# A four-layer transformer kernel: projections split on two engines, fewer query transfers, and turnings in another order

## The reference

```python
# layers 0, 1 and 3 (norms and gates differ a little)
x = x + gate1 * proj(self_attention(ln(x)))
x = x + proj(cross_attention(q=x_or_ln(x), kv=context))
x = x + gate2 * mlp(ln(x))
# layer 2, a router over three experts
nx = ln(x); q = nx @ Wq; k = context @ Wk; v = context @ Wv
weights = softmax(q @ k.T * 128 ** -0.5)
evidence = weights @ v
combined = concat(nx, evidence, cond)
x = x + sigmoid(gate(combined)) * out(sum_e prob_e * expert_e(combined))
```

## Time and profile before

| | us |
|---|---|
| median of 3 runs | 6248.7 (6243.0 to 6251.5) |
| the profiled execution | 6255.5 |
| its span, first to last instruction | 6253.2 |
| mean granted TensorE clock | 0.881 |

### The profile page before, as it was taken

How to read it: one execution, slowest core, us unless ns; L and a number is a source line. 1 busy time by engine, 2 the same in 40 slices (tenths; PEclk the granted TensorE clock), 3 DMA queues, 4 the chain that set the end, 5 groups by cost and what they waited for, 6 DMA issues and landing times. The chain is left out here.

```text
span 6253.2 us, 151177 instructions
## 1 busy us (share of the span) xinstructions
PE 5213.4 (83%) x64126; PEld 3352.7 (54%) x64126; DVE 3844.1 (61%) x7732; ACT 3016.4 (48%) x4479; POOL 1458.3 (23%) x758
## 2 busy tenths in 40 slices
PE   4838999999985849999999877779675799999998
PEld 3614555555653615666666545555353466666664
DVE  4537888888744527777777623334353577777773
ACT  2324666666652315666666532212322366666665
POOL 2024444444302022333222000000201223332220
PEclk7667999999996669999999977779766799999999
DMA  3325545555403345555555211110141555555540
GB/s 76 63 64 156 158 157 164 164 164 158 147 17 65 64 110 162 165 164 165 164 167 164 73 33 48 48 38 1 44 77 28 171 165 165 165 164 164 164 152 15
DMA packets 544827, 717.59 MB, mean 115 GB/s; under 512 B 183450, under 2 KB 457402, under 8 KB 531770
## 3 DMA queue, kind: packets, MB, share of 16 engines
q1 hardware_dynamic: 535322, 696.87, 38.4%
q10 hardware_dynamic: 8832, 11.07, 0.8%
HBM read 441.82 MB, written 264.09 MB: 113 GB/s over the span
## 5 line engine op out<-in xcount | busy, mean ns | idle before, releaser
L1247 DVE TENSOR_REDUCE maxima<-ps 100x1 f32<-100x482 f32 (+1 forms) x4608 | 2720.2, 650 | 896.3 <-PE ps L1092 886.6
L1202 ACT ACTIVATE probs<-ps 128x800 f32<-128x800 f32 (+1 forms) x2304 | 1800.5, 835 | 655.6 <-PE ps L1113 653.9
L1092 PE MATMUL ps<-kst,qst 48*100 48x482 bf16 (+1 forms) x4608 | 1117.7, 411 | 107.1 <-DMA qst<-cross_q_parts 51.3
L1299 POOL TENSOR_TENSOR kparts<-kf,zero 128x1444 bf16<-128x1444 f32 x192 | 498.3, 2595 | 2280.3 <-ACT kf L1174 2250.9
L1130 PE MATMUL ps<-probs,vals 128*9 128x100 f32 x36864 | 1012.4, 250 | 7.9 <-ACT probs L1202 0.8
L1113 PE MATMUL ps<-qst,kst 128*128 128x200 bf16 (+1 forms) x9216 | 999.6, 250 | 11.7 <-DMA qst<-nparts 5.5
L1113 PEld LDWEIGHTS ps<-qst,kst 128*128 128x128 bf16 (+1 forms) x9216 | 759.0, 98 | 251.2 <-issue 124.7
L1130 PEld LDWEIGHTS ps<-probs,vals 128*9 128x9 f32 x36864 | 734.3, 90 | 259.6 <-issue 219.2
L1092 PEld LDWEIGHTS ps<-kst,qst 48*100 48x100 bf16 x4608 | 341.7, 119 | 630.2 <-DVE maxima L1247 329.9
L1180 ACT ACTIVATE vals<-ps 128x512 f32<-128x512 f32 (+1 forms) x288 | 161.9, 562 | 467.1 <-PE ps L1075 467.1
L1064 PE MATMUL ps<-ident,ctok 128*128 128x128 f32 (+1 forms) x1152 | 195.6, 292 | 210.2 <-DMA ctok<-in_ctx_dram 108.7
(11 more groups left out here) (256 smaller groups left out, 4951.3 us busy)
## 6 DMA issues: line engine op xcount, KB each, us to landing
kst<-ctx_k_stack SPq DMA_DIRECT2D x96, 2888.0 KB
ctx_k_stack<-kparts SPq DMA_DIRECT2D x192, 541.5 KB
ctx_k_stack<-kparts SPq DMA_DIRECT2D x192, 361.0 KB
ctok<-in_ctx_dram SPq DMA_DIRECT2D x96, 704.0 KB
ctx_k_stack<-kparts SPq DMA_DIRECT2D x192, 180.5 KB
c<-in_ctx_dram SPq DMA_DIRECT2D x32, 704.0 KB
o_sums<-osb SPq DMA_DIRECT2D x96, 200.0 KB
qst<-cross_q_parts SPq DMA_DIRECT2D x1152, 12.5 KB
```

The costliest lines, as they stand in the source:

```text
L1092: nc.tensor.matmul(ps[0:N, at:at + w], g.qst[s][row0:row0 + CROWS, j, N * e:N * e + N], g.kst[s][row0:row0 + CROWS, j, a:a + w], start=Tru ...
L1202: nc.scalar.activation(probs[kt % 2][hf][0:kts[kt], :].rearrange("p (k n) -> p k n", k=2), src, ACT.Exp).then_inc(exp_done, 1)
L1247: nc.vector.reduce_max(maxima[:, col:col + 1], ps[0:N, at:at + widths[c]], AX.X).then_inc(m_read, 1)
L1299: return nc.gpsimd.tensor_tensor(out, src, g.zero[0:src.shape[0], 0:1].to_broadcast(list(src.shape)), ALU.add)
```

## The change

It has three parts.

1. The splitting. A class `Split` says which chunks are "banked". Banked chunks are scaled in place in their PSUM bank and subtracted there by VectorE (rest to the bank, low to `parts[:, 2]`); the others go through `sq` and GpSimd as before. In a stage with two projections the first has no banked chunk and the second has all eight; in a stage with one projection the even chunks are banked. VectorE and ScalarE interleave the steps by chunk: VectorE scaling of c, rest of c - 1, low of c - 2; ScalarE high of c, middle of c - 1. GpSimd does the rest of a chunk and then the low part of the one before. The second projection no longer waits for the low parts of the first.
2. The query transfers. `cross_q_parts` gets the shape (8 chunks, 2, 3, 64, 400), and SyncE stores two transfers per chunk, 16 in a stage. The loads of cross attention read each batch's 100 columns out of rows of 400.
3. The router attention. The turning of context and weights is taken out of `pe_scores` and `pe_evidence`. TensorE's order per batch becomes: weights groups 0 and 1 of b, context groups 0 and 1 of b + 2, weights group 2, context group 2, evidence of b, scores of b + 2. The order on the other engines stays.

```diff
+class Split:
+    def __init__(self, sem, i, banked, parts, f):
+        self.banked, self.parts, self.f = banked, parts, f
+        self.f_ready, self.high, self.middle = sem(f"proj_read{i}"), sem(f"high{i}"), sem(f"middle{i}")
...
+    def value(self, g, c):
+        return bank(g, c) if c in self.banked else tok(self.f, c)
...
+def dve_split(g, dve, s, full, bias, scale):
+    for c in range(NCH + 2):
+        if c < NCH:
+            dve.wait_ge(full, c + 1)
+            g.nc.vector.tensor_scalar(s.value(g, c), bank(g, c), bias, scale, ALU.add, ALU.mult).then_inc(s.f_ready, 1)
+        if 0 <= c - 1 < NCH and c - 1 in s.banked:
+            dve.wait_ge(s.high, c)
+            g.nc.vector.tensor_tensor(bank(g, c - 1), bank(g, c - 1), s.part(0, c - 1), ALU.subtract).then_inc(s.dve_rest, 1)
+        if 0 <= c - 2 < NCH and c - 2 in s.banked:
+            dve.wait_ge(s.middle, c - 1)
+            g.nc.vector.tensor_tensor(s.part(2, c - 2), bank(g, c - 2), s.part(1, c - 2), ALU.subtract).then_inc(s.dve_low, 1)
+
+
+def act_split(g, act, s):
+    for c in range(NCH + 1):
+        if c < NCH:
+            act.wait_ge(s.f_ready, c + 1)
+            g.nc.scalar.activation(s.part(0, c), s.value(g, c), ACT.Copy).then_inc(s.high, 1)
+        if c:
+            act.wait_ge(s.rest(c - 1), s.nth(c - 1))
+            g.nc.scalar.activation(s.part(1, c - 1), s.value(g, c - 1), ACT.Copy).then_inc(s.middle, 1)
+
+
+def pool_split(g, pool, s):
+    copied = [c for c in range(NCH) if c not in s.banked]
+    for c, before in zip(copied + [None], [None] + copied):
+        if c is not None:
+            pool.wait_ge(s.high, c + 1)
+            g.nc.gpsimd.tensor_tensor(tok(s.f, c), tok(s.f, c), s.part(0, c), ALU.subtract).then_inc(s.pool_rest, 1)
+        if before is not None:
+            pool.wait_ge(s.middle, before + 1)
+            g.nc.gpsimd.tensor_tensor(s.part(2, before), tok(s.f, before), s.part(1, before), ALU.subtract).then_inc(s.pool_low, 1)
...
-    per = CH // N
     for c in range(NCH):
-        sp.wait_ge(low, c + 1)
+        sp.wait_ge(split.low(c), split.nth(c))
         for e in range(2):
-            for j in range(per):
-                b = c * per + j
-                sp.dma_start(g.qx[b, e].rearrange("t r n -> r t n"),
-                             parts[HALF * e:HALF * e + HALF, :, N * b:N * b + N]).then_inc(stored, 16)
-    sp.wait_ge(stored, 16 * 2 * B)
+            sp.dma_start(g.qx[c, e].rearrange("t r n -> r t n"),
+                         parts[HALF * e:HALF * e + HALF, :, CH * c:CH * c + CH]).then_inc(stored, 16)
+    sp.wait_ge(stored, 16 * 2 * NCH)
...
+        banked = [(), tuple(range(NCH))] if npart == 2 else [tuple(range(0, NCH, 2))]
+        splits = [Split(sem, i, banked[i], parts[i], sq) for i in range(npart)]
...
+            per = CH // N
             for e in range(2):
                 for part, (first, copies) in enumerate(Q_SLOTS):
+                    src = g.qx[b // per, e, part].rearrange("(d j) n -> d j n", j=PAIRS)[:, :, N * (b % per):N * (b % per) + N]
                     for slot in range(first, first + copies):
                         at = QHALF * e + HD * slot
-                        sp.dma_start(g.qst[s][at:at + HD, :, N * e:N * e + N],
-                                     g.qx[bass.ds(b, 1), e, part].rearrange("a (d j) n -> (a d) j n", j=PAIRS)).then_inc(qst_loaded[s], 16)
+                        sp.dma_start(g.qst[s][at:at + HD, :, N * e:N * e + N], src).then_inc(qst_loaded[s], 16)
...
+                for b in range(B):
+                    k, k2 = known(b), known(b + 2) if b + 2 < B else None
+                    for t in range(2):
+                        pe_turn_weights(pe, k, t)
+                    if k2 is not None:
+                        for t in range(2):
+                            pe_turn_context(pe, k2, t)
+                    pe_turn_weights(pe, k, 2)
+                    if k2 is not None:
+                        pe_turn_context(pe, k2, 2)
+                    pe_evidence(pe, k)
+                    if k2 is not None:
+                        pe_scores(pe, k2)
```

More of the change, by code:

```diff
@@ L163, in act_shift @@
         g.nc.scalar.activation(tok(xn, b, N), tok(xn, b, N), ACT.Identity, bias=add[:, bass.ds(b, 1)]).then_inc(modulated, 1)
-def act_split(g, act, f, parts, f_ready, high, rest, middle):
-    for c in chunks(act):
-        act.wait_ge(f_ready, c + 1)
-        g.nc.scalar.activation(parts[:, 0, bass.ds(c * CH, CH)], tok(f, c), ACT.Copy).then_inc(high, 1)
-    for c in chunks(act):
-        act.wait_ge(rest, c + 1)
-        g.nc.scalar.activation(parts[:, 1, bass.ds(c * CH, CH)], tok(f, c), ACT.Copy).then_inc(middle, 1)
@@ L176, in pool_split @@
-def pool_split(g, pool, f, parts, high, rest, middle, low):
-    for c in chunks(pool):
-        pool.wait_ge(high, c + 1)
-        g.nc.gpsimd.tensor_tensor(tok(f, c), tok(f, c), parts[:, 0, bass.ds(c * CH, CH)],
-                                  ALU.subtract).then_inc(rest, 1)
-    for c in chunks(pool):
-        pool.wait_ge(middle, c + 1)
-        g.nc.gpsimd.tensor_tensor(parts[:, 2, bass.ds(c * CH, CH)], tok(f, c),
-                                  parts[:, 1, bass.ds(c * CH, CH)], ALU.subtract).then_inc(low, 1)
@@ L188, in sp_parts_out, with part, nth, rest @@
-def sp_parts_out(g, sp, parts, dram, low, stored):
+class Split:
+    def __init__(self, sem, i, banked, parts, f):
+        self.banked, self.parts, self.f = banked, parts, f
+        self.f_ready, self.high, self.middle = sem(f"proj_read{i}"), sem(f"high{i}"), sem(f"middle{i}")
+        self.dve_rest, self.pool_rest = sem(f"dve_rest{i}"), sem(f"pool_rest{i}")
+        self.dve_low, self.pool_low = sem(f"dve_low{i}"), sem(f"pool_low{i}")
+    def part(self, k, c):
+        return self.parts[:, k, CH * c:CH * c + CH]
+    def value(self, g, c):
+        return bank(g, c) if c in self.banked else tok(self.f, c)
+    def nth(self, c):
+        return len([x for x in range(c + 1) if (x in self.banked) == (c in self.banked)])
+    def rest(self, c):
+        return self.dve_rest if c in self.banked else self.pool_rest
+    def low(self, c):
+        return self.dve_low if c in self.banked else self.pool_low
@@ L395, in project_phase @@
         full = [sem(f"proj_full{i}") for i in range(npart)]
-        f_ready = [sem(f"proj_read{i}") for i in range(npart)]
-        high = [sem(f"high{i}") for i in range(npart)]
-        rest = [sem(f"rest{i}") for i in range(npart)]
-        middle = [sem(f"middle{i}") for i in range(npart)]
-        low = [sem(f"low{i}") for i in range(npart)]
+        banked = [(), tuple(range(NCH))] if npart == 2 else [tuple(range(0, NCH, 2))]
+        splits = [Split(sem, i, banked[i], parts[i], sq) for i in range(npart)]
         stored = [sem(f"stored{i}") for i in range(npart)]
@@ L421, in _ @@
                     pe_linear(g, pe, [w], [lambda c: tok(xin, c)], xin_ready, xin_per, free, full[i])
-                    free = f_ready[i]
+                    free = splits[i].f_ready
             @block.vector
@@ L435, in _ @@
                 for i, (w, bias, dram, scale) in enumerate(projections):
-                    for c in chunks(dve):
-                        dve.wait_ge(full[i], c + 1)
-                        if i:
-                            dve.wait_ge(low[i - 1], c + 1)
-                        nc.vector.tensor_scalar(tok(sq, c), bank(g, c), bias, scale, ALU.add,
-                                                ALU.mult).then_inc(f_ready[i], 1)
+                    dve_split(g, dve, splits[i], full[i], bias, scale)
             @block.scalar
@@ L453, in _ @@
                 for i in range(npart):
-                    act_split(g, act, sq, parts[i], f_ready[i], high[i], rest[i], middle[i])
+                    act_split(g, act, splits[i])
             @block.gpsimd
@@ L458, in _ @@
                 for i in range(npart):
-                    pool_split(g, pool, sq, parts[i], high[i], rest[i], middle[i], low[i])
+                    pool_split(g, pool, splits[i])
             @block.sync
@@ L464, in _ @@
                     if dram is g.qx:
-                        sp_queries_out(g, sp, parts[i], low[i], stored[i])
+                        sp_queries_out(g, sp, parts[i], splits[i], stored[i])
                     else:
-                        sp_parts_out(g, sp, parts[i], dram, low[i], stored[i])
+                        sp_parts_out(g, sp, parts[i], dram, splits[i], stored[i])
 class attention_close_sems:
```

59 lines of the change are left out of this document (28 added, 31 removed).

## The result

The changed kernel takes 6003.2 us (median of 4 runs, 5998.3 to 6009.0) against 6249.8 for the kernel before in the same session: ratio 0.9608, 95% interval 0.9591 to 0.9624. That is 247 us less, where 221 was forecast. The profiled executions took 6255.5 and 6009.0 us, spans 6253.2 and 6007.2, so 246.0 us are to be found in the traces.

| stretch | before | after | gained | forecast |
|---|---|---|---|---|
| three query stages | 164.1 | 56.3 | 107.9 | 110 |
| three self projection stages | 105.7 | 92.3 | 13.4 | 6 |
| router attention, first query copy to the next block's first product | 502.5 | 378.4 | 124.1 | 105 |
| everything else | | | 0.6 | 0 |

The account below looks back on a forecast made before the run. Bounds named: SyncE's issuing queue in query stages, GpSimd in self stages, a chain through TensorE in the router. Gains of 110 + 6 + 105 = 221 us from 6248.7 gave 6028 us, range 5985 to 6105.

Parts of the forecast that it names:

- Part 1: Query stages: 16 transfers and the new split take three stages from 164.1 to 54.3 us, gain 110 (99 to 119).
- at 1.0 to 1.3 us a chunk the queue keeps up: Query stages: SyncE's issues, 0.51 to 0.65 us each, keep pace with the split, which is late next.
- 4.14: Query stages: us from the last transfer's start to the stage's end, taken from the self stage.
- Part 2: Self projection stages: VectorE alone splits the second projection; gain 2.2 us each, 6 in all (bounds -6 and 12).
- Part 3: Router attention: slot 10.5 us at full clock, 11.7 with the clock's cost; gain 105 us (46 to 144).
- clock surcharge: Router attention: the mean slot's 3.20 us above full clock falls to 1.2, bounds 0 to 3.20.
- The load that the move exposes: Router attention: TensorE waits some 0.8 us for the context's load, hidden at full clock behind the stall for VectorE's copy.
- Part 4: Cross attention's query loads: strided reads issue in the same 0.646 us; no change, bounds -0.1 and +0.1 us an issue.
- (a): Router attention: the order helps but the clock costs the same; slot 13.7, gain 46, total 6087 us; chance 0.17.
- (b): Router attention: the clock falls in every slot; slot 16.1, 24 us lost, total 6157 us; chance 0.11.
- (c): Cross attention: SyncE issues strided query loads more slowly; at 1.6 us an issue, total 6527 us; chance 0.03.
- (d): Splits: part 2 gains nothing, part 1 its lower bound; 17 us less, total 6045; chance 0.67 together with the forecast.

Follow-up runs that it names:

- The run with eight transfers: The changed kernel with both self projections split by alternate chunks between VectorE and GpSimd, and one query transfer per chunk: 5978.3 us, ratio 0.9560 to before.
- copies first: The kernel before, with VectorE copying a batch's turned weights ahead of the maximum over the next batch's scores: 6114.2 us, ratio 0.9776.
- gap filled: The kernel before with two needless products per router slot in TensorE's 1.75 us wait: 6153.4 us; with ten needless turnings instead: 6172.1 us.
- a fourth buffer: The changed kernel with a fourth context buffer in the router attention, so contexts load a slot earlier: 6036.5 us, ratio 0.9647 to before.
- a third less of it: The changed kernel with a fourth context buffer and one needless product per slot behind the context's second group: 6038.0 us, ratio 0.9646 to before.
- the router without stalls: The changed kernel with four context buffers and reordered router work on VectorE, ScalarE and TensorE: 5914.4 us, ratio 0.9456 to before.

## Why the prediction was right, and where its sizes were off

**Part 1, query stages: right, for a reason partly wrong.** The split ends 11.2 to 12.4 us after the first scaling (forecast 12.3 to 13.0) and a pair of chunks takes 2.17 us (369.27 to 371.44 from one scaling to the next but one), not 2.55. The step that failed is "at 1.0 to 1.3 us a chunk the queue keeps up": a chunk takes 1.09 us and two issues some 1.3 (0.617 each, 0.66 from one to the next), so the queue is late again; its last issue ends 4 us behind the last low part in place of 1.3. The run with eight transfers shows the price: 2.6 us a stage. Two errors went the other way: the split was 0.75 us shorter on average, and what follows the last issue takes 2.9 us, where the sum had 4.14. It had taken these 4.14 from the start of the self stage's last issue and counted both issues besides, one of them twice. So 56.3 us against 54.3 is luck in part.

**Part 2, self stages: mechanism right, a term mis-sized.** ScalarE came free 14.9 us after the first scaling (84.11 against 69.26; forecast 15.0), and VectorE had waited 8.00 us for it. But then a chunk took 1.50 us, not 1.86, and the last low part came at 26.6 in place of 29.1; 13.4 us were gained, over my upper bound of 12. I had read 0.664 as what a scaling costs VectorE. It was TensorE's pace: two instructions per chunk, some 0.33 us apart. The 0.60 for a subtraction was too long as well. Among work that is ready a scaling takes 0.54 and a subtraction 0.48 from start to start, less than the 0.63 and 0.57 that the rows give as durations. The Trainium skill (Perfetto Trace Analysis, DVE / Act Engine Instruction) says why one may not add these: the profiler's end is the acknowledgement of the write, and the next instruction may begin once the one before has finished executing. The trace agrees, by the 0.09 us between 0.57 and 0.48.

**Part 3, router: full-clock slot right (10.36 against 10.5), clock surcharge mis-sized.** Of the 4.31 us a slot gained, 1.76 are the shorter slot at full clock (forecast 1.6; 1.50 of it are stalls, 3.39 to 1.89, and 0.26 busy time of TensorE, 8.73 to 8.47) and 2.55 clock (forecast 2.0): the surcharge fell from 3.20 to 0.65 where I took 1.2. The term that was mis-sized is that 1.2; it makes 16 of the 19 us by which this part did better. The idle time ahead of the evidence came out nearly as forecast, 1.89 against 1.8. Of the two reasons given, that stalls shrink and that a stretch without a break follows, the first is shown by itself (copies first; gap filled), and the second isn't needed for it. But "the cause shrinks" doesn't make a scale: with a fourth buffer the same idle time costs 1.43 us a slot in its fastest execution, and with a third less of it 1.90, the two kernels being equal by medians. My bounds of 0 to 3.20 were fair; that I placed the value by an amount of idle time was more luck than reading.

The load that the move exposes was named rightly and hidden as said (10.37 us in the slot from 3863.43 on, which has no such wait), but the wait was 1.5 to 2.1 us and not 0.8:

```profile
3845.63 0.38 SPq L1604 DMA_DIRECT2D c<-in_ctx_dram  x1
...
3850.57 1.09 PE L1615 MATMUL ps<-ident,c 128*128 128x128 f32 x8 [1.69 <-DMA c<-in_ctx_dram]
```

From the issue to the turning there were 4.9 us; the last bytes on the wires at 3845.90 to 3846.40, 4.0 to 4.5 us after the issue, were a lower end.

**Part 4: right.** The strided loads are issued in the same time as the earlier trace rows:

```profile
L1385 SPq DMA_DIRECT2D qst<-cross_q_parts x1152: 632/647/1799, 427.2 to 5828.1; - x192
```

**The rivals.** (a), the clock costs what it did: refuted, 0.65 in place of 3.20 us. (b), it falls in every slot: refuted, six of 29, although each slot opens with 4.8 us of turnings and waits; the two kernels with a fourth buffer (13 and 17 of 29) would fit a weaker form of its mechanism, but don't show it. (c), longer issues: refuted by the row above. (d), the splits do less: together they did more, 121 us against 116.

**The range.** Its lower end, 5985, was added up with 133 us for the router, where the bound given for that part is 144 (4.8 us times 30 slots); with 144 it is 5974. The result lies inside either.

**Open.** Why 1.89 us of idle time goes with six long slots in one arrangement and with 13 or more in another, and 1.24 with 17, when 1.16 beside products and 1.05 in the order of before go with none. For the order of before the runs show that the idle time before the evidence was the cause. For the new order they show that its amount and place don't decide alone (with the fourth buffer, equal slots come out short and long), and that without any (the router without stalls, which is also shorter) no slot is long; they don't give the rule.

## What to carry to other kernels

Where TensorE's clock falls again and again at the same wait, count the fall and not only the wait: here 1.75 us of waiting cost 3.2 us more in clock, and the cheapest cure was to move one call on another engine. In the order of before it was enough to make the gap smaller (1.75 to 0.33 or 0.44 us). In the new order neither moving nor shrinking it helped, and only the kernel that left no gap at all had no long slot; so read the clock again after each such move. When work goes to another engine, take its cost from start to start among work that is ready, and compare the queue that follows with the new pace, not with the old.

## What was not expected of the hardware

- Needless products in a wait made a kernel 104 us faster (6257 to 6153), through the clock alone.
- To remove a hidden wait of 1.6 us for a load made the changed kernel slower, by 24 us by ratio (0.9608 to 0.9647 of before) and 33 by medians (6003 to 6036).
- Back to back on a PSUM bank, VectorE starts a 400-column subtraction every 0.48 us and a scaling 0.54 us ahead of the next, with durations of 0.57 and 0.63 in the same rows.
